# One piece of tensor-engine work for the weighted sums of two key tiles, in a planned two-layer transformer kernel

## What is computed

```python
dots = jnp.einsum('bhid,bhjd->bhij', q, k) * SCALE
attn = jax.nn.softmax(dots, axis=-1)
out = jnp.einsum('bhij,bhjd->bhid', attn, v)
```

## Time and profile before

| what | us |
|---|---|
| median of 3 runs | 1126.51 (1124.65 to 1131.03) |
| span of the profiled execution | 1128.5 |
| PE busy in it | 1008.6 |
| DVE busy | 868.6 |
| ACT busy | 722.5 |
| POOL busy | 431.7 |

### The profile page before, as it was taken

One profiled execution on the slowest core, in us unless ns is written; L12 is line 12 of the kernel. 1 busy time (PEld: TensorE's weight loads), 2 busy tenths in 40 slices (PEclk: granted clock), 3 DMA queues, 4 the chain that ended last, 5 costly groups with the idle time before them and its releaser, 6 DMA issues.

```text
span 1128.5 us, 22542 instructions
## 1 busy us (share of the span) xinstructions
PE 1008.6 (89%) x8315; PEld 533.8 (47%) x8315; DVE 868.6 (77%) x1814; ACT 722.5 (64%) x1112; POOL 431.7 (38%) x484
## 2 busy tenths in 40 slices
PE   4589899899999898999989899898989899899986
PEld 2122222224555453555556575555656555355554
DVE  3898989898878687987747887679867677886465
ACT  4057777677766675666656565565755678577763
POOL 3000212344033535510544543563361167835463
PEclk9568998889999899999989999999999999999998
DMA  4814443456756566455467676568658748511110
GB/s 137 173 34 120 121 100 105 128 155 192 222 184 199 168 201 184 146 165 166 162 192 202 209 192 225 160 185 271 182 190 231 221 140 219 131 58 56 64 31 19
DMA packets 122509, 176.06 MB, mean 156 GB/s; under 512 B 20280, under 2 KB 86200, under 8 KB 122400
## 3 DMA queue, kind: packets, MB, share of 16 engines
q1 hardware_dynamic: 116064, 161.24, 49.0%
q0 software_dynamic: 5760, 12.59, 3.8%
q10 hardware_dynamic: 576, 0.79, 0.3%
HBM read 114.77 MB, written 59.67 MB: 155 GB/s over the span
## 4 chain that ended last, share of the span: by engine, by line
PE 42%; DVE 18%; DMA 18%; issue 9%; POOL 8%; ACT 4%; SPq 1%; POOLq 0%; DVEq 0%; ACTq 0%
PE ps L808 11%; DVE nm L1001 10%; PE ps L870 7%; DMA gr<-d_y,pos 5%; PE ps L791 5%; PE ps L769 5%; DMA d_h<-hx,pos 4%; PE ps L892 3%; DMA d_h<-r,pos 3%; PE ps L916 2%; DMA d_r<-DC 2%; POOL gr L1563 2%; DMA DR<-d_r 1%; ACT xn L1296 1%; PE ps L909 1%
## 5 line engine op out<-in xcount | busy, mean ns | idle before, releaser
L1001 DVE TENSOR_REDUCE nm<-ps 128x2 f32<-128x1024 f32 (+3 forms) x512 | 502.1, 1017 | 90.8 <-PE ps L774 44.0
L1355 ACT ACTIVATE ES<-ps 128x1024 f32<-128x1024 f32 (+1 forms) x448 | 420.1, 962 | 146.3 <-PE ps L791 81.8
L808 PE MATMUL ps<-ES,VS 128*9 128x512 f32 (+3 forms) x2048 | 227.1, 531 | 0.2
L769 PE MATMUL ps<-KS,QS 48*128 48x512 bf16 (+3 forms) x1024 | 178.1, 367 | 42.3 <-DVE nm L1001 17.6
L791 PE MATMUL ps<-QS,KS 51*128 51x512 bf16 (+3 forms) x1024 | 171.4, 353 | 19.6 <-DVE nm L1001 9.3
L870 PE MATMUL ps<-hsT,wst 128*128 128x128 f32 x1104 | 154.2, 286 | 7.2 <-DVE nm L1001 4.6
L870 PEld LDWEIGHTS ps<-hsT,wst 128*128 128x128 f32 x1104 | 135.9, 194 | 39.2 <-issue 28.1
L1563 POOL DMA_INDIRECT gr<-d_y,pos x80 | 83.6, 1045 | 130.4 <-DMA gr<-d_y,pos 60.3
L769 PEld LDWEIGHTS ps<-KS,QS 48*128 48x128 bf16 x1024 | 49.8, 95 | 171.5 <-DVE nm L1001 59.5
L791 PEld LDWEIGHTS ps<-QS,KS 51*128 51x128 bf16 x1024 | 50.2, 94 | 154.8 <-DVE nm L1001 48.2
L1388 ACT ACTIVATE tx<-ps 128x384 f32<-128x384 f32 x92 | 45.2, 491 | 40.2 <-PE ps L870 36.4
(11 more groups left out here) (200 smaller groups left out, 1491.4 us busy)
## 6 DMA issues: line engine op xcount, KB each, us to landing
wst<-we SPq DMA_DIRECT2D x92, 576.0 KB
d_u<-US SPq DMA_DIRECT2D x64, 256.0 KB
KS<-d_k SPq DMA_DIRECT2D x64, 192.0 KB
QS<-d_q SPq DMA_DIRECT2D x64, 192.0 KB
hs<-d_h SPq DMA_DIRECT2D x25, 256.0 KB
d_y<-ys SPq DMA_DIRECT2D x25, 256.0 KB
d_q<-sp SPq DMA_DIRECT2D x16, 384.0 KB
d_k<-sp SPq DMA_DIRECT2D x16, 384.0 KB
```

The source lines that it names most:

```text
L769: mm = eng.matmul(psum[:, bank[u][a], c:c + n], QS[m][r:r + KA, pr, 128 * t1:128 * t1 + 128], KS[m][r:r + KA, pr, 0:n], start=True, stop=i ...
L808: mm = eng.matmul(psum[32 * a:32 * a + 9, b, q0:S], VS[i % 3][:, j1, 4 * g + a, :], ES[(2 * EXP[i, g, j] + a // 2) % NES][:, a % 2, c:c + ...
L1001: ins = eng.tensor_reduce(nm[f][:, :].rearrange("p (a c) -> p a c", a=2)[:, :, 4 * pr + t1], ps2("score", i, f, pr, t)[:, :, c:c + n], AX. ...
L1355: eng.activation(ES[(2 * n + pp) % NES][:, :, 0:w], ps2("bscore", i, f, g, j, pp)[:, :, 0:w], ACT.Exp, scale=SC1 if i >= NB else SC0).then ...
```

## The change

It does five things. (1) Two neighbouring key tiles of one (i, g) become one pv piece: 0 and 1, then 2 and 3 (layer 1: 0 and 1, then 2 alone). The piece is named after its second tile and costs the sum of both. It waits for the exponentials of each of its tiles in turn. Whoever waited for the pv of one tile now waits for the piece that holds it (`joined`). (2) The bank of a group is opened by its first piece, ("pv", i, g, 1). (3) The prices of a change of mode are a table, one price for each pair of modes, in place of 0.2 into "full" and 0.1 into the others, and the handicap in the choice is the same for all changes of mode. (4) The offsets of the urgencies are other numbers, larger, for more families and batches. (5) The semaphore values of `t_gt` follow from the batch and no longer from the place in the queue; batch 15 has a semaphore of its own.

```diff
-SHIFT = {"t": -0.11, "s": 1.11, "p": -0.35, "stack": -0.35, "pv": 0.21, "f": 0.37, "d": 1.32, "x": 1.09, "max": -0.38, "r": 0.26, "rr": 0.26, "u": -0.15, "g": -0.9, "bscore": -0.08, "expo": -0.08}
+SHIFT = {"bscore": -0.08, "c": 0.23, "d": 2.23, "expo": -0.11, "f": 0.39, "g": -1.96, "ld": -10.94, "max": -0.39, "p": -0.35, "pv": 0.21, "r": 1.3, "rr": 0.27, "s": 1.02, "stack": -4.24, "t": -0.32, "u": -0.56, "w": 0.19, "x": 1.09}
...
-LATE = {"d": 0.03, "f": -0.28, "score": 0.02, "rowmax": 0.02, "t": 0.59, "max": 0.24, "g": -0.08, "u": 0.23, "s": -0.66, "x": 0.07}
+LATE = {"c": -2.56, "d": -0.11, "expo": 0.36, "f": -4.15, "g": -5.56, "ld": -2.62, "m": -6.08, "max": 0.12, "pv": 0.02, "r": 8.16, "rowmax": 0.01, "rr": -9.08, "s": -4.06, "score": 0.02, "stack": -2.35, "t": 0.97, "u": 2.27, "w": -10.77, "x": -1.6}
...
 NUDGE = {
-    "p": [-0.59, 1.36, 2.69, 0.58, 0.41, 0.15, -0.14, -0.36, -0.4, 0.0, 0.0, 0.21, -0.12, -0.16, -0.31, -1.81],
+    "p": [-4.25, 4.39, 9.5, 0.45, 1.63, 0.33, -0.14, -0.88, -0.32, 0.0, 0.01, 0.19, -0.12, -0.19, -1.55, -9.25],
...
-    "max": [-1.09, -0.97, 0.08, 0.16, -0.77, -1.33, -1.41, -1.06, -0.07, -0.03, -1.66, -1.04, -1.58, -0.72, -5.31, 1.12],
+    "max": [-13.1, -13.76, -8.88, -9.08, -7.62, -7.82, -2.29, -0.28, -4.58, 0.07, -3.26, -5.55, -7.63, -11.1, -18.21, -7.31],
...
-                    sw = (0.2 if m == "full" else 0.1) if e == "PE" and m != mode and w else 0.0
+                    sw = SWITCHES.get((mode, m), 0.1) if e == "PE" and m != mode and w else 0.0
...
-                t, sw, urg, k = min((f for f in fit if f[0] <= t0 + SLACK), key=lambda f: f[2] + SWITCH * (2 if f[1] > 0.15 else f[1] > 0))
+                t, sw, urg, k = min((f for f in fit if f[0] <= t0 + SLACK), key=lambda f: f[2] + SWITCH * (f[1] > 0))
...
+SWITCHES = {("full", "half"): 0.1, ("full", "cols"): 0.1, ("half", "full"): 0.08, ("half", "cols"): 0.08,
+            ("cols", "full"): 0.11, ("cols", "half"): 0.113}
...
+def joined(k):
+
+    i, g, j = k
+    return (i, g, min(j | 1, KEYS[i][-1]))
...
-                old = [("pv",) + EXPS[m]] if m >= 0 else []
+                old = [("pv",) + joined(EXPS[m])] if m >= 0 else []
...
-                add("PE", ("pv", i, g, j), 0.008 + 0.857 * n / 512, u + 0.06, exps[-2:] + [("p_vs", i)] + ([("pv", i, g, j - 1)] if j else []), mode="cols", opens=int(j == 0))
+                if j == joined((i, g, j))[2]:
+                    two = range(j // 2 * 2, j + 1)
+                    add("PE", ("pv", i, g, j), sum(0.008 + 0.857 * width(i, m) / 512 for m in two), u + 0.06, exps[-2 * len(two):] + [("p_vs", i)]
+                        + ([("pv", i, g, 1)] if j > 1 else []), mode="cols", opens=int(j == 1))
...
-                "t_ld": (1, 1), "t_gt": (2, 1), "x_ld": (2, 1), "x_st": (2, 1), "g_gc": (1, 1), "m_st": (2, 1), "m_ld": (2, 2)}
+                "t_ld": (1, 1), "t_gt": (3, 1), "x_ld": (2, 1), "x_st": (2, 1), "g_gc": (1, 1), "m_st": (2, 1), "m_ld": (2, 2)}
...
+            if k[0] == "t_gt":
+                return (s["t_gt", k[1] % 2], 16 * (k[1] // 2 + 1)) if k[1] < N - 1 else (s["t_gt", 2], 16)
...
-                    for j1, c, q0 in key_tiles(i, j):
-                        for a in range(4):
-                            q.wait_ge(*on("expo", i, g // 2, g % 2, j, a // 2))
...
+                    for m in range(j // 2 * 2, j + 1):
+                        for j1, c, q0 in key_tiles(i, m):
+                            for a in range(4):
+                                q.wait_ge(*on("expo", i, g // 2, g % 2, m, a // 2))
...
                     if n >= NES // 2:
-                        q.wait_ge(*on("pv", *EXPS[n - NES // 2]))
+                        q.wait_ge(*on("pv", *joined(EXPS[n - NES // 2])))
```

More of the change, by code:

```diff
@@ L69, in wait_ge @@
             self.seen[sem.name] = value
-SHIFT = {"t": -0.11, "s": 1.11, "p": -0.35, "stack": -0.35, "pv": 0.21, "f": 0.37, "d": 1.32, "x": 1.09, "max": -0.38, "r": 0.26, "rr": 0.26, "u": -0.15, "g": -0.9, "bscore": -0.08, "expo": -0.08}
-LATE = {"d": 0.03, "f": -0.28, "score": 0.02, "rowmax": 0.02, "t": 0.59, "max": 0.24, "g": -0.08, "u": 0.23, "s": -0.66, "x": 0.07}
-LAST = {"max": -1.22, "r": -0.08, "rr": -0.08, "pv": 0.15, "u": 1.18, "d": 0.41, "score": -0.01, "rowmax": -0.01, "g": -0.13, "bscore": -0.01, "expo": -0.01, "t": 0.82, "x": 0.66, "s": 0.21}
+SHIFT = {"bscore": -0.08, "c": 0.23, "d": 2.23, "expo": -0.11, "f": 0.39, "g": -1.96, "ld": -10.94, "max": -0.39, "p": -0.35, "pv": 0.21, "r": 1.3, "rr": 0.27, "s": 1.02, "stack": -4.24, "t": -0.32, "u": -0.56, "w": 0.19, "x": 1.09}
+LATE = {"c": -2.56, "d": -0.11, "expo": 0.36, "f": -4.15, "g": -5.56, "ld": -2.62, "m": -6.08, "max": 0.12, "pv": 0.02, "r": 8.16, "rowmax": 0.01, "rr": -9.08, "s": -4.06, "score": 0.02, "stack": -2.35, "t": 0.97, "u": 2.27, "w": -10.77, "x": -1.6}
+LAST = {"bscore": -0.01, "c": -0.17, "d": 0.83, "expo": 1.14, "f": 1.0, "g": -0.82, "ld": 1.31, "m": 2.04, "max": -9.16, "p": 0.01, "pv": -1.47, "r": -12.93, "rowmax": 4.95, "rr": -2.47, "s": -1.2, "score": -0.01, "stack": -5.84, "t": 0.41, "u": -6.97, "w": -7.88, "x": 3.55}
 NUDGE = {
-    "p": [-0.59, 1.36, 2.69, 0.58, 0.41, 0.15, -0.14, -0.36, -0.4, 0.0, 0.0, 0.21, -0.12, -0.16, -0.31, -1.81],
-    "score": [-0.01, -0.05, -0.01, 0.0, 0.0, 0.0, 0.09, -0.04, 0.0, 0.0, 0.0, -0.08, -0.01, 0.05, 0.09, 0.37],
-    "max": [-1.09, -0.97, 0.08, 0.16, -0.77, -1.33, -1.41, -1.06, -0.07, -0.03, -1.66, -1.04, -1.58, -0.72, -5.31, 1.12],
-    "expo": [-0.1, -0.01, 0.0, 0.0, 0.0, 0.0, 0.0, 0.0, 0.0, 0.0, -0.04, -0.53, -0.01, -0.04, 0.2, -0.09],
[9 rows of a table removed]
+    "p": [-4.25, 4.39, 9.5, 0.45, 1.63, 0.33, -0.14, -0.88, -0.32, 0.0, 0.01, 0.19, -0.12, -0.19, -1.55, -9.25],
+    "score": [-0.78, -0.05, -0.01, 0.0, 0.01, -0.0, -0.0, -0.05, -0.0, -0.0, -0.1, 0.12, -0.01, 0.1, 0.11, 0.35],
+    "max": [-13.1, -13.76, -8.88, -9.08, -7.62, -7.82, -2.29, -0.28, -4.58, 0.07, -3.26, -5.55, -7.63, -11.1, -18.21, -7.31],
+    "expo": [-3.8, -0.01, 0.0, -0.26, -0.0, -0.0, -0.0, -0.0, -0.0, 0.0, -0.05, -5.16, -0.01, -0.04, 0.31, -2.28],
[9 rows of a table added]
 }
@@ L355, in plan @@
                     exps.append(("expo", i, f, g % 2, j, pp))
-                add("PE", ("pv", i, g, j), 0.008 + 0.857 * n / 512, u + 0.06, exps[-2:] + [("p_vs", i)] + ([("pv", i, g, j - 1)] if j else []), mode="cols", opens=int(j == 0))
-            add("ACT", ("u_copy", i, g), 0.49, u + 0.1, [("pv", i, g, KEYS[i][-1]), ("u_st", i - (g < 2), (g - 2) % NG)], closes=[("pv", i, g, 0)])
+                if j == joined((i, g, j))[2]:
+                    two = range(j // 2 * 2, j + 1)
+                    add("PE", ("pv", i, g, j), sum(0.008 + 0.857 * width(i, m) / 512 for m in two), u + 0.06, exps[-2 * len(two):] + [("p_vs", i)]
+                        + ([("pv", i, g, 1)] if j > 1 else []), mode="cols", opens=int(j == 1))
+            add("ACT", ("u_copy", i, g), 0.49, u + 0.1, [("pv", i, g, KEYS[i][-1]), ("u_st", i - (g < 2), (g - 2) % NG)], closes=[("pv", i, g, 1)])
             add("SP", ("u_st", i, g), 0.4, u + 0.1, [("u_copy", i, g)], lag=2.4)
@@ L670, in slot @@
         def slot(*k):
+            if k[0] == "t_gt":
+                return s["t_gt", k[1] % 2 if k[1] < N - 1 else 2]
             return s[k[0], (nth[k] - 1) % DMAS[k[0]][0]]
@@ L801, in _ @@
                     q.wait_ge(*on("p_vs", i))
-                    if j == 0:
+                    if j == 1:
                         open_banks(u)
-                    b = bank["pv", i, g, 0][0]
-                    for j1, c, q0 in key_tiles(i, j):
-                        for a in range(4):
-                            q.wait_ge(*on("expo", i, g // 2, g % 2, j, a // 2))
-                            mm = eng.matmul(psum[32 * a:32 * a + 9, b, q0:S], VS[i % 3][:, j1, 4 * g + a, :],
-                                            ES[(2 * EXP[i, g, j] + a // 2) % NES][:, a % 2, c:c + S - q0],
-                                            start=(j1 == 0), stop=(j1 == NT - 1), skip_group_check=True)
+                    b = bank["pv", i, g, 1][0]
+                    for m in range(j // 2 * 2, j + 1):
+                        for j1, c, q0 in key_tiles(i, m):
+                            for a in range(4):
+                                q.wait_ge(*on("expo", i, g // 2, g % 2, m, a // 2))
+                                mm = eng.matmul(psum[32 * a:32 * a + 9, b, q0:S], VS[i % 3][:, j1, 4 * g + a, :],
+                                                ES[(2 * EXP[i, g, m] + a // 2) % NES][:, a % 2, c:c + S - q0],
+                                                start=(j1 == 0), stop=(j1 == NT - 1), skip_group_check=True)
                     mm.then_inc(s["pv"], 1)
@@ L1361, in _ @@
                         q.wait_ge(*on("u_st", i - (g < 2), (g - 2) % NG))
-                    eng.activation(US[g % 2][:, :], ps("pv", i, g, 0), ACT.Copy).then_inc(s[k], 1)
+                    eng.activation(US[g % 2][:, :], ps("pv", i, g, 1), ACT.Copy).then_inc(s[k], 1)
                 elif k == "f_exp":
```

## The result

The changed kernel takes 1147.4 us (median of 4 runs, 1143.73 to 1159.4) where the kernel before took 1125.58 beside it: a ratio of 1.0187, 95% interval 1.0124 to 1.0251. The forecast was 1095, range 1070 to 1131. It is slower by 1.9%, clear of no change, and outside the range.

The account below looks back on a forecast made before the run. PE was taken to bound the kernel from 85 to 1050 us. Visits -15, idle time -12 and clock -5 sum to -32 us: span 1128.5 to 1096.5, median 2.0 below, so 1095 us, range 1070 to 1131.

Parts of the forecast that it names:

- Added or moved in the pieces: nothing on PE: Pv pieces on PE: longer holds make exponentials wait, but ACT's slack covers it; cost 0.
- Rival 1: Pv at the head of PE's list waits for its second tile's exponentials, 43 times 0.86 us; 1148 us, chance 0.17.
- The visits: PE's visits to the column mode: at least 86 of 214 fall away, a gain of 15 us.
- The prediction's own sign of being wrong: On PE: the prediction is wrong if the visits fall and PE's busy time does not; 15 to 25 us less was expected.
- The prices: Planner's mode prices and equal handicap: changes between full and half on PE, taken at 0, 9 us either way.
- The offsets: Order of all engines, middle of the kernel: 12 us less idle time on PE and 5 us from its clock.
- The bound of a loss of 36 us: PE's idle time if all the middle ran as 700 to 800 us does: 108 us, against 72.
- The stages: Split of the timeline; 85 to 1050 us taken as PE's stretch, PE busy 893.1 of 965 us, DVE 762.4.
- The start and the tail: First batch's row maxima on a full DVE, and last batch's chain: 0 each, the tail bounded by PE's 15 us idle.
- the loads and t_gt: SP's queue: earlier loads taken at 0, 10 us either way; new semaphore values of t_gt add no transfer, 0.

Follow-up runs that it names:

- e7: Kernel before with the two key tiles of 95 pairs put next to each other in PE's list alone; 1152.05 us, ratio 1.019.
- e4: Changed kernel, order untouched, with pv's semaphore raised after each key tile; 1152.22 us, ratio 1.0179 to the kernel before.
- e16: Kernel before with 22 first tiles of batches 0 to 4 moved back to the second, plus a ninth ES buffer; ratio 1.0113.
- e9: Kernel before with 56 pairs, those of batches 5 to 15 alone, put next to each other in PE's list; 1133.62 us, ratio 1.001.
- e13: Kernel before with the first tile of 22 pairs in batches 0 to 4 moved back to the second in PE's list; ratio 1.0077.
- e14: Kernel before with the second tile of 17 pairs in batches 0 to 4 moved forward to the first in PE's list; ratio 1.0041.
- e3: Kernel before with the new table of mode prices and the equal handicap alone; 1169.44 us, ratio 1.030.
- e5: Changed kernel with the offsets of before, pairs and new prices kept; 1187.51 us, ratio 1.049 to the kernel before.
- e10: Kernel before with row maxima and exponentials over half of their columns, leaving out part of the attention; 1097.79 us.
- e11: Kernel before with 95 pairs put together in PE's list, and row maxima and exponentials over half of their columns; 1110.8 us.

## Why the prediction was wrong

- **The step that failed** is "Added or moved in the pieces: nothing on PE", of which the prediction says "I cost it at 0". e7 puts pairs into the order of before, with no new offset and no new price, and loses 1.9%, 21 us; up to the end of batch 4 it has lost 24. The step looked for the cost at the exponentials that wait for pv, found ACT's slack there, and was right about that place: e4 and e16 show no cost in the buffers. It did not ask what else a pv piece holds up. Behind it on PE stand score and bscore, for which DVE and ACT wait. And on ACT `u_copy` waits for it; in the kernel before it already did so 25 times:

```profile
ACT US L1362 <- PE ps L808: 21.6, 25, 2.5
```

That pairs cost this much in batches 0 to 4 is shown; by which of these two ways is open.
- **Rival 1** had the sign and the size (1148 us), and the wrong place, so that its size fits is luck: it came from 43 waits of 0.86 us at pv. Pv itself hardly waits in the changed kernel; the page has 1.3 us of idle time before L824 in all, and score and bscore are what waits. The strict order of matmuls that the Trainium skill gives (TensorE: Matmul & The Clock Gate, The mechanism) fits the timeline above, where no score passes a pair:

```profile
L824 PE MATMUL ps<-ES,VS 128*9 128x512 f32 (+3 forms) x2048 | 211.5, 533 | 1.3 <-DVE nmp L1029 0.6
```

- **The visits** fell by 88 where at least 86 were forecast, and a pair holds PE for 1.84 us as priced. The 15 us were taken to lie "on the path as long as PE does", and no run shows them as a gain. The prediction's own sign of being wrong came true: the visits fall and PE's busy time does not. In e7 it is 1009.0 us at a clock of 0.951, before 1008.6 at 0.949, with 157 changes of mode fewer. e9 saves 49 visits in batches 5 to 15 for no gain. PE is busy for 94% of 85 to 365 us, and yet time saved on its visits there did not shorten the span (e7, e13, e14).
- **The prices** were taken at 0 with 9 us either way. The 77 additional changes between full and half are at the end of that range, 8 us. What the range left out is that a new price is a new order: e3 is 3.0% slower with 18 more such changes.
- **The offsets** were to bring 12 us of idle time and 5 of clock; the kernel lost about 12 and up to 21. The bound of a loss of 36 us held. The step's reason, that truer prices let the planner take away waits, did not carry it: both plans lose 5 to 6% by one random draw of up to a tenth of a batch, so the old offsets were already closely fitted to their plan, and the new ones start from a plan of 1187 us (e5), not of 1126.
- **The stages** were weighed by the mean of 85 to 1050 us. Batches 0 to 4 have DVE at 87%, later ones at 74%. Read apart, the first stretch would have been a warning that DVE has little slack to hide a pair behind; e10 and e11 show that this is not the whole of it.
- The start and the tail, taken at 0, changed by a few us: the first 128 pv records end at 117.7 us in place of 115.4, and the last pv lies 60 us before the end of the span in place of 59. No run isolates the loads and t_gt.
- Two slips in the working changed nothing: the 128 pieces come from 64 groups in all, 32 of each layer; and 17 + 25 + 10 us off 1126.5 give 1074.5, not 1073.

Open is which part of the 35 us up to the end of batch 4 in the changed kernel is the pair's and which is its order's. e7 has 24 us there with an order that was not worked out for pairs; single tiles in batches 0 to 4 with pairs behind them, and offsets worked out for that, were not tried. Nor was an order of ACT in which `u_copy` comes one or two exponentials later.

## What to carry to other kernels

On an engine that works in turn with two others through a few buffers, a piece is also a time for which it does not serve them. Before making pieces longer to save changes of mode, look stage by stage at everyone who waits for them or for what stands behind them, in every engine's list, and not only at the wait that comes to mind first. And where an order has been fitted, price a change of the planner against the fit that is lost: run it once with a meaningless jitter, which here cost 6%, twice what was to be gained.

## What the runs showed of the hardware that was not expected

That the granted clock falls to 1.2 GHz after waits that are each under a microsecond was seen in the earlier trace rows already; what was not expected is how much oftener it falls. It stands at that level in 22 stretches of the changed kernel, and in 13 of the kernel before. Ahead of the fall at 248.8 us PE had waited 0.74, 0.36 and 0.52 us between pieces in half mode and was busy for 5.34 of 7.0 us; then a pair took 3.05 us in place of 1.84. Idle time and a lower clock went together in these runs: the changed kernel with the jitter has 50 us more outside PE's busy time than before (170.0 against 119.9), and at a clock of 0.902 in place of 0.949 the same matmuls keep PE busy for 39 us more (1048.0 against 1008.6). It is 7.4% slower.
